# A two-feed-forward, one-attention block on one core: output banks emptied in one go, two norms swapped, q and k given slots of their own

## What is computed

```python
x = x + 0.5 * ffn(layernorm(x), W1, W2, W3)     # W1, W3: 2048 x 512, W2: 512 x 2048
x = x + attn(layernorm(x), qkv_w, ...)          # 16 heads of 32, chunks of 128 tokens
x = x + 0.5 * ffn(layernorm(x), W1, W2, W3)

def ffn(x, W1, W2, W3):
    hidden = silu(x @ W1.T) * (x @ W3.T)
    return fwht(hidden) @ W2.T                  # Walsh-Hadamard transform of the hidden values

def attn(x, ...):
    h = rmsnorm(x) * qkv_norm_w
    q, k, v = h @ ternary(qkv_w).T              # per head and chunk of 128 tokens:
    scores = (q @ k.T) * mask                   # mask: exp(-s * (t - t')) for t >= t'
    o = scale * (scores @ v + (q * lam_t) @ S)
    S = lam_T * S + (k * lam_rev).T @ v         # state carried from chunk to chunk
    return rmsnorm(rmsnorm(o) * norm_w) @ ternary(proj_w).T
```

## Time and profile before

| | |
|---|---|
| median of 3 runs | 2386.85 us (2386.35 to 2392.28) |
| the profiled execution | 2383.02 us, of it the span 2381.3 us |
| PE matmuls busy | 2299.9 us, 97% of the span |
| DVE busy | 1570.3 us, 66% |
| ACT busy | 905.7 us, 38% |
| POOL busy | 214.2 us, 9% |
| DMA engines, mean busy share | q1 45.2% |

### The profile page before, as it was taken

The page is one execution under the profiler, slowest core; times in us unless marked ns, Lnnn a source line. Parts: engine busy times, 40 slices in busy tenths (PEclk is TensorE's granted clock), DMA queues, the critical chain, the costliest instruction groups (busy, mean ns, idle before and its releaser), DMA issues. The chain is left out here.

```text
span 2381.3 us, 48863 instructions
## 1 busy us (share of the span) xinstructions
PE 2299.9 (97%) x19551; PEld 1782.2 (75%) x19551; DVE 1570.3 (66%) x3540; ACT 905.7 (38%) x1877; POOL 214.2 (9%) x206
## 2 busy tenths in 40 slices
PE   9999999999999999899999999999999998999998
PEld 5444444678887888778877887788777886878887
DVE  7677456666776667657675677666676666666544
ACT  7645133333343334234433343333333333333322
POOL 0380033100000000000000000000000000000000
PEclk9999999999999999999999999999999999999999
DMA  9865533452544334544372344532544445243322
GB/s 242 226 161 164 140 102 94 154 127 76 138 131 147 89 92 126 149 110 111 85 193 76 107 111 143 128 99 76 180 101 113 107 110 138 85 118 85 109 89 65
DMA packets 351714, 291.57 MB, mean 122 GB/s; under 512 B 253824, under 2 KB 278656, under 8 KB 348672
## 3 DMA queue, kind: packets, MB, share of 16 engines
q1 hardware_dynamic: 351056, 287.66, 45.2%
q10 hardware_dynamic: 432, 0.79, 0.1%
HBM read 173.02 MB, written 59.77 MB: 98 GB/s over the span
## 5 line engine op out<-in xcount | busy, mean ns | idle before, releaser
L1919 PE MATMUL d_bank<-w2t,work 128*128 128x256 f16 x2496 | 377.6, 274 | 24.0 <-DVE work L1554 9.5
L1505 DVE SCALAR_TENSOR_TENSOR work<-l_bank,l_scale,work 128x256 f32<-128x256 f32 x416 | 181.6, 478 | 250.5 <-PE l_bank L1887 248.6
L1887 PE MATMUL g_bank<-work,w1t 128*128 128x256 f16 x2688 | 315.8, 275 | 2.0 <-ACT work L1151 2.0
L1887 PE MATMUL l_bank<-work,w3t 128*128 128x256 f16 x2688 | 313.4, 273 | 0.1
L1887 PEld LDWEIGHTS g_bank<-work,w1t 128*128 128x128 f16 x2688 | 264.0, 99 | 40.5 <-ACT work L1151 2.1
L1887 PEld LDWEIGHTS l_bank<-work,w3t 128*128 128x128 f16 x2688 | 262.8, 98 | 34.1 <-DVE work L1505 0.4
L1919 PEld LDWEIGHTS d_bank<-w2t,work 128*128 128x128 f16 x2496 | 236.5, 98 | 62.2 <-issue 12.1
L1919 PE MATMUL d_bank<-work 128*128 128x256 f16 x1872 | 274.5, 274 | 0.0
L1887 PE MATMUL l_bank<-xt,w3t 128*128 128x256 f16 x2304 | 268.7, 273 | 0.0
L1887 PE MATMUL g_bank<-xt,w1t 128*128 128x256 f16 x2304 | 267.2, 273 | 1.2 <-ACT work L1151 0.9
L1522 DVE TENSOR_TENSOR work<-work 128x256 f16<-128x256 f32 (+1 forms) x416 | 256.9, 618 | 15.1 <-ACT work L1163 11.8
(11 more groups left out here) (287 smaller groups left out, 2954.2 us busy)
## 6 DMA issues: line engine op xcount, KB each, us to landing
work<-w_dram SPq DMA_DIRECT2D x208, 384.0 KB, 3.4
work<-parts_dram SPq DMA_DIRECT2D x192, 128.0 KB, 2.9
x_dram<-work SPq DMA_DIRECT2D x16, 1024.0 KB, 4.8
parts_dram<-q_parts SPq DMA_DIRECT2D x32, 256.0 KB, 2.0
parts_dram<-k_parts SPq DMA_DIRECT2D x32, 256.0 KB, 2.3
norm_dram<-cent SPq DMA_DIRECT2D x32, 256.0 KB, 2.2
w2t<-in_L_ffn_W_dram SPq DMA_DIRECT2D x31, 256.0 KB, 3.4
xin<-in_L_attn_x_dram SPq DMA_DIRECT2D x7, 1024.0 KB, 8.0
```

The lines of the kernel that those rows point to most:

```text
L1505: nc.vector.scalar_tensor_tensor(out=tokens, in0=l_bank[:, HALF * e:HALF * (e + 1)], scalar=l_scale[:, tile:tile + 1], in1=tokens, op0=ALU ...
L1887: ins = nc.tensor.matmul(dst[:, HALF * e:HALF * (e + 1)], wt[:, wp, k, P * tile:P * (tile + 1)], f.x[:, s_half, xp, k, :], start=(k == 0 a ...
L1919: ins = nc.tensor.matmul(bank_m[:, cols], combos[:, q % 2, hp, combo, :], weights[:, wp, :], start=(p == 0 and opens and hp == wp), stop=( ...
```

## The change

The diff has five parts.

1. **Banks in one go.** `hend` is gone. `hout` on DVE now makes all seven evictions behind each other (`evict`), and the residual rows are added to them there (`src`). POOL's two additions come after them and work in place: it adds `u_sums[:, 0]` to the first rows after the fourth eviction, and `u_sums[:, 1]` to the second rows after the seventh. DVE waits for the first of them ahead of its seventh eviction. PE waits for evictions 2, 3, 5 and 7 at its four bank openings. The steps of slot+2 stand behind the evictions instead of between them.
2. **The attention norm ahead of the output norm.** The norm "ffn2" of batch b moves from ahead of the attention norm of batch b+1 to six slots behind its start. Its bn_stats stand among the steps of the attention norm. The attention's heads start 18 slots after the norm's start (14 before), the first q 9 slots after it (7 before).
3. **q and k in slots of their own.** For groups 1 to 3, k moves from 5 to 11 slots ahead of its head, q from 7 to 4. `kturn` moves from 2 to 6 slots ahead (4 for group 0), and its last subtraction becomes a step `kdlow`, 2 slots ahead. `sclow` stands one slot after its `score`.
4. **Fewer operations.** The attention norm's second pass over the tile (L1644) is gone: `rstd` is applied by ACT's cast and by DVE's `split`. ACT writes k's high half straight from the bank, and DVE its low half from the bank as for q; so `k` holds its bank for two copies, and `kT` no longer holds k. Three multiplications of 128 columns in `kturn` become one of 384.
5. A few `unpark` steps and the norm ("ffn1", 7) move by 4 to 13 slots.

```diff
-                        steps += [("hdown", (0, PAIRS - 1)), ("hout", 0)] + slots.get(slot + 2, [])
-                        steps += [("hend", 0), ("resid", 0), ("resid", 1)]
+                        steps += [("hdown", (0, PAIRS - 1)), ("hout", 0), ("resid", 0), ("resid", 1)] + slots.get(slot + 2, [])
...
+                heads = [first + 18 + GROUP_PERIOD * g for g in range(GROUPS)]
+                for g, at in enumerate(heads):
+                    add(slots, at, [("kv", (b, g)), ("score", (b, g, 0)), ("state", (b, g))])
+                    add(slots, at + 1, [("sclow", (b, g, 0)), ("statestore", (b, g)), ("statespread", (b, g))])
+                    for c in range(1, TT):
+                        add(slots, at + 2 * c, [("score", (b, g, c))])
+                        add(slots, at + 2 * c + 1, [("sclow", (b, g, c)), ("pv", (b, g, c - 1))])
+                    add(slots, at + 9, [("pv", (b, g, TT - 1))])
+                for g, at in enumerate(heads):
+                    k_at, q_at = (at - 11, at - 4) if g else (at - 7, at - 9)
+                    add(slots, k_at, [("k", (b, g))])
+                    add(slots, k_at + 1, [("klow", (b, g))])
+                    add(slots, q_at, [("q", (b, g))])
+                    add(slots, q_at + 1, [("qlow", (b, g))])
+                    add(slots, q_at + (2 if g else 3), [("qspread", (b, g))])
+                    add(slots, at - 5, [("kspread", (b, g))])
+                    add(slots, at - 6 if g else at - 4, [("kturn", (b, g))])
+                    add(slots, at - 2, [("kdlow", (b, g))])
...
+                out_norm = first + PERIOD + 6 if b < B - 1 else end + 10 + TT
...
-            return {"q": (0, 2), "k": (0, 1), "score": (0, 1), "kv": (1, 1)}.get(step)
+            return {"q": (0, 2), "k": (0, 2), "score": (0, 1), "kv": (1, 1)}.get(step)
...
+                    pool.wait_ge(u_done, OUTS * h + 4)
+                    nc.gpsimd.tensor_tensor(dst[:, first_rows, HALF:D], dst[:, first_rows, HALF:D], u_sums[:, 0],
                                             ALU.add).then_inc(rows_added, 1)
...
+                    pool.wait_ge(u_done, OUTS * h + (5 if n == 2 * B - 1 else 7))
+                    two = dst[:, second_rows].rearrange("p (c d) -> p c d", c=2)
+                    nc.gpsimd.tensor_tensor(two, two, u_sums[:, 1:2].to_broadcast([P, 2, HALF]), ALU.add).then_inc(res_done, 2)
...
+                    evict(first_rows, left, p6_p1, src)
...
                     dve.wait_ge(d_ready, down + 3)
...
+                    evict(first_rows, right, p4_p5, src)
+                    evict(second_rows, slice(0, D), p4_p5, src)
                     dve.wait_ge(d_ready, down + 4)
...
+                    dve.wait_ge(u_done, OUTS * h + 2)
+                    evict(first_rows, left, p2_p3, dst)
+                    dve.wait_ge(rows_added, h + 1)
+                    evict(first_rows, right, p2_p3, dst)
...
-                        ins = nc.vector.tensor_scalar(to, to, rstd[:, t:t + 1], None, ALU.mult)
+                        ins = nc.vector.scalar_tensor_tensor(out=to, in0=src, scalar=mean[:, t:t + 1], in1=qnw_row[:],
+                                                             op0=ALU.subtract, op1=ALU.mult)
```

More of the change, by code:

```diff
@@ L55, in macaron_kernel @@
     COMBOS = 7
+    OUTS = 7
     ctx = ExitStack()
@@ L350, in fast_feed_forward @@
             if last:
-                steps += [("hdown", (1, PAIRS - 1)), ("hout", 1), ("hend", 1), ("resid", 2), ("resid", 3)]
+                steps += [("hdown", (1, PAIRS - 1)), ("hout", 1), ("resid", 3), ("resid", 2)]
             return steps
@@ L371, in attention_slots @@
             for b in range(B):
-                at = FIRST_NORM + PERIOD * b
+                first = FIRST_NORM + PERIOD * b
                 if 0 < b < B - 1:
[L374 to L401, removed]
@@ L402, in attention_slots @@
-                add(slots, end + 1, [("ostat", (b, 0)), ("ostat", (b, 1))])
+                    add(slots, first - 11, [("fetch", b)])
+                norm(first, ("qkv", b))
+                heads = [first + 18 + GROUP_PERIOD * g for g in range(GROUPS)]
[6 more added lines that the diff above has]
+                    add(slots, at + 9, [("pv", (b, g, TT - 1))])
@@ L406, in attention_slots @@
                     add(slots, end + 9 + t, [("proj", (b, t))])
-                add(slots, end + 1, [("projload", b)])
                 add(slots, end + 9 + TT, [("keep", b)])
+                out_norm = first + PERIOD + 6 if b < B - 1 else end + 10 + TT
                 for t in range(TT):
-                    add(slots, end + 10 + t, [("rows", (("ffn2", b), t))])
-                norm(end + 9 + TT, ("ffn2", b))
+                    add(slots, out_norm - 5 + t if b < B - 1 else end + 10 + t, [("rows", (("ffn2", b), t))])
+                norm(out_norm, ("ffn2", b))
             add(slots, 4, [("early", 3)])
@@ L1176, in _ @@
                         act.wait_ge(flipped[t % 2], flips(key, t) - 16)
-                    nc.scalar.copy(halves[:, t % 2, 0, :], centred).then_inc(ln_hi, 1)
+                    if key[0] == "qkv":
+                        nc.scalar.activation(halves[:, t % 2, 0, :], centred, ACT.Copy, scale=rstd[:, t:t + 1]).then_inc(ln_hi, 1)
+                    else:
+                        nc.scalar.copy(halves[:, t % 2, 0, :], centred).then_inc(ln_hi, 1)
                 elif step == "prep" and arg[1] == 3:
@@ L1534, in _, with evict @@
                     wait_for_rows(dve, f, s_half)
-                    nc.vector.scalar_tensor_tensor(out=dst[:, first_rows, 0:HALF], in0=p6_p1[:, 0:HALF], scalar=ffn_unscale[:],
-                                                   in1=src[:, first_rows, 0:HALF], op0=ALU.mult, op1=ALU.add).then_inc(u_done, 1)
+                    left, right = slice(0, HALF), slice(HALF, D)
+                    def evict(rows, cols, bank, added):
+                        nc.vector.scalar_tensor_tensor(out=dst[:, rows, cols], in0=bank[:, cols], scalar=ffn_unscale[:],
+                                                       in1=added[:, rows, cols], op0=ALU.mult, op1=ALU.add).then_inc(u_done, 1)
@@ L1832, in _ @@
                             continue
+                        elif f.which == "ffn2":
+                            pe.wait_ge(flipped2[f.batch % 2], 16 * TT * (f.batch // 2 + 1))
                         else:
```

101 lines of the change are left out of this document (43 added, 58 removed).

## The result

The changed kernel takes **2314.6 us** in the median of 4 runs (2312.4 to 2315.6), the kernel before 2386.6 beside it: a ratio of 0.9694, 95% interval 0.9675 to 0.9713. The forecast of 2326.5 was 12 us too high, and the time lies inside the range. The total is nearly right; several parts are not, and the experiments show that part 1, the banks, costs time inside the whole change where it was to save 12 us.

What follows compares the result with a forecast made beforehand. PE's own work (2299.9 of 2381.3 us) bounds the kernel, with its waits and the clock as the rest. Terms sum to -60.3 us: 2383.0 profiled to 2322.7, plus 3.8 for the median gives 2326.5 us, range 2298 to 2362.

Steps and rivals of the forecast that it cites:

- The first q: PE's 22.7 us wait for the transposed norm at a batch's first q falls to 2: -20.7 us (-22.7 to -11).
- The banks: PE's 15.2 us of `hdown` waits for banks DVE has yet to empty fall to 3: -12 us (-15 to -4).
- slower rival: Evictions make DVE's next product (L1505) and low halves late, some 4.7 us in each of 26 halves: 2449 us; 5%.
- kv: `kv`'s 8.0 us wait for the decayed k goes, since k starts 11 slots ahead: -8 us (-8 to -4).
- q, pv and score: Waits of q, k and `pv` for a bank or low halves, 9.1 us, mostly go: -7 us (-9 to +3).
- hlow and gate: Waits of `hdown` and `hgate` for DVE's low half and ACT's cast, 8.2 us: -4 us (-6 to 0).
- The W2 fetch: PE's 3.2 us wait for one late fetch of W2 stays, as its store and load do: 0 (-3 to +5).
- The operations: Removed DVE passes (32 x 0.49 us), ACT copies and merged multiplications are work beside PE: 0 by itself.
- The clock: Of ten half-clock stretches in the matmuls' time three stay; 8 x 1.7 us saved: -13.6 us (-17 to -7).
- New waits: POOL's second addition beside DVE costs at most 0.8 us at each of 26 halves: +5 us (0 to 21).
- signs of being wrong: New PE waits on DVE's L1503 or L1508 products, spread parts of q, or W2's fetches in place of old ones.
- The rule from the Trainium skill: A VectorE instruction with two SBUF inputs and a GpSimd one reading SBUF exclude each other for a whole instruction.

Runs made afterwards that it cites:

- the old exchange ahead of the steps: Changed kernel with DVE again waiting for POOL's additions between its evictions, but `hend` right behind `hout`, ahead of the slot's steps: 2323.2 us, ratio 0.974.

## Why the prediction was right in the total and wrong in its parts

One path from before to the changed kernel was measured step by step: 2386.1, with norm swap and distance 2366.7 (-19), with the slots of q, k and the low halves 2314.4 (-52), with fewer operations 2306.6 (-8), with the new banks 2314.6 (+8). The prediction's list gave 20.7, 15, 0 and 12 us to these four, and the clock and new waits apart.

- **The first q, -20.7: right.** 22.7 us of waits went to none. The sum counted the distance and that is borne out: the swap without it gave nothing (21.8 us of the wait stayed), the two together take the wait away. Whether the swap is needed was not run.
- **The banks, -12: the step that failed.** The sum asked how soon DVE frees the banks and found PE's cover long enough, which the trace confirms: the seven evictions took 3.1 us (3.6 in the sum), and no wait for them is left. It priced the new order as if nothing that PE needs stood behind the evictions. The prediction named DVE's product as what could be late, in its slower rival; what was late was ACT, held at the norm's cast ahead of the gate's activation. Part 1 is worth -4.7 us in the old slots and +8 in the new, by runs.
- **kv, -8: right in size, by luck in the reason.** 8.0 us went to no wait, but the swap with the distance alone had brought it to 3.2, and with q and k back in their old slots only 1.2 came back. The early k, which the term was built on, is worth little of it.
- **q, pv and score, -7: mis-sized as the worth of the slots.** With the heads moved by four, the rest of the slot table carries 52 us. Of it the slots of q and k cost 12.7 when undone in the changed kernel; the rest stays open between the low halves' slots, which the prediction named only as a small cost, and the parts together. The prediction weighed all this against the waits of before, while most of the 38.4 us of waits that they remove only arise once the heads have moved. The waits that it took from the earlier trace rows did nearly go; 5.9 us for q's bank came up in two places.
- **hlow and gate, -4: wrong sign at the gate.** `hlow` went from 5.3 to 2.1 us, the gate from 2.9 to 8.7: 8.2 became 10.8.
- **The W2 fetch, 0:** 3.2 to 1.1 us, not followed up.
- **The operations, 0: mis-sized.** "Work beside PE" was worth 8 us in the new slots with the old banks, and the centring's pass alone 6 in the changed kernel, where the gate waits and those for q's bank grow with it.
- **The clock, -13.6: right.** 0.992 to 0.997 is 0.005 x 2312 = 12 us, and with the clocks that the traces give before rounding, 0.9916 and 0.9974, it is 13.9.
- **New waits, +5: mis-sized.** The term stood for POOL's second addition beside DVE: the price per instruction was right (1.44 us for a `split` of 0.75), and the addition cut short gave 7.4 us. The new waits in PE's list are more than that: gate +5.8 (counted above already), q's bank +5.9, `proj` 2.9, together 14.6 us. The ones that the prediction named as signs of being wrong (DVE's products, spread parts of q, the W2 fetch) did not come.

How these cancel shows in the balance. Without the clock the sum had 60.3 - 13.6 = 46.7 us; PE's empty time fell by 47.0. Too much hope in the banks was made up by too little in the smaller waits. PE's busy time fell by 21.9 us instead of the 13.6 of the clock; these 8.3, and the 3.4 us by which the median stands nearer to the profiled execution than before (0.4 us above it, not 3.8), are the 12 us of error. The 8.3 are no faster matmuls. A batch's modelled end lies past the next one's start, as in these rows of PE in the changed kernel:

```profile
738.12 0.49 PE L1915 MATMUL d_bank<-w2t,work 128*128 128x256 f16 x3
738.45 0.82 PE L1915 MATMUL d_bank<-work 128*128 128x256 f16 x6
```

738.12 + 0.49 is 738.61, 0.16 us after 738.45. So the first 0.16 us of each wait count as busy. PE's whole list of before holds 62 waits (52 of them in the earlier trace rows), the one of after 21, and 41 x 0.16 makes 6.6 us of the 8.3; the rest stays open.

The rule from the Trainium skill (SBUF — State Buffer, "Who interferes with whom") that spoke against part 1 held: a `split` with two SBUF inputs took 1.44 us beside POOL's addition and 0.75 in the median. But it hardly tells part 1 from the old exchange. With the banks undone the `split` at the same place is stretched as well, and before it was L1641:

```profile
736.00 1.38 DVE L1660 SCALAR_TENSOR_TENSOR cent<-cent,rstd 128x512 f16<-128x512 f32 x1
```

So the 7.4 us of the shortened addition are what the overlap costs in the changed kernel, and not what part 1 added to it. What part 1 costs is its order, 16.7 us, as the old exchange ahead of the steps shows, and its exchange gives 8.6 of that back.

## What to carry to other kernels

Before you put a block of work in one piece on an engine, write down what it pushes back, and on every engine whose in-order queue has an instruction waiting for that: here ACT stood idle for 6 us with the activation that PE needed behind a cast. A part that pays alone can cost inside the whole change, so undo each part in the finished kernel: the changed kernel without its first part is 8 us faster (2306.6 us) than with it. And when several orders end at the same time with another bank late each time, look whether the local engine is full: DVE was busy 7.22 of 7.61 us there. If it is, try to take work out, as the single pass of the centring did, instead of moving it.

## What was not expected of the hardware

- One instruction of 0.49 us that VectorE no longer does, 32 times (13.1 us of its work with what goes along), gave 6.2 us of a span in which VectorE is busy 67%: an engine's mean share says nothing about the pairs in which it is the last to finish.
- Moving a chain of steps by four slots brought 12.4 us of waits for the DMAs that spread q and k, one of 6.2 us, with the same transfers; the slot table moves only when they are issued. What else of the move made them late is not shown.
- A wait of 3.26 us in the changed kernel was followed by 24 matmuls in 4.43 us that take 2.62 at full clock: 1.8 us on top of the wait. The granted clock from 743.80 to 748.30 is 0.62, so part of that stretch went at 1.2 instead of 2.4 GHz, and 0.38 x 4.5 = 1.7 us were lost. It agrees with the 1.7 us per stretch that the prediction took from the windows.
